# Sixteen-head attention and routed experts: VectorE adds the rotation products itself, and the row maximum is split around the additions

## The reference

```
xn = layernorm(x)
q = rope((xn  @ Wq.T + bq) as 16 heads of 8)
k = rope((ctx @ Wk.T + bk) as 16 heads of 8)
v = (ctx @ Wv.T + bv) as 16 heads of 8
p = softmax(where(mask, q k^T / sqrt(8), -1e9))
x = x + tanh(g_x) * ((p v) @ Wo.T + bo)

xn = layernorm(x);  e = argmax(xn @ Wr + br);  g = softmax(...)[e]
x = x + tanh(g_f) * g * (gelu(xn @ W1[e] + b1[e]) @ W2[e] + b2[e])
```

## Time and profile before

| | |
|---|---|
| median of 3 runs | 280.02 us (279.95 to 280.26) |
| the profiled execution, its own time | 283.1 us |
| span from first to last instruction | 281.2 us |
| busy: TensorE, VectorE, ScalarE, GpSimd | 83%, 68%, 59%, 65% |
| mean granted TensorE clock | 0.983 |

### The profile page before, as it was taken

The page is one execution under the profiler, slowest core; times in us unless marked ns, Lnnn a source line. Parts: engine busy times, 40 slices in busy tenths (PEclk is TensorE's granted clock), DMA queues, the critical chain, the costliest instruction groups (busy, mean ns, idle before and its releaser), DMA issues.

```text
span 281.2 us, 10499 instructions
## 1 busy us (share of the span) xinstructions
PE 234.1 (83%) x3529; PEld 203.5 (72%) x3529; DVE 191.5 (68%) x639; ACT 167.2 (59%) x484; POOL 182.7 (65%) x222
## 2 busy tenths in 40 slices
PE   1357898989799898787897899588889999999992
PEld 1235777878578777666776787477778899999992
DVE  5545777888789979998778977868568434434430
ACT  1235678878577787666886777626473434444440
POOL 7374755757646889746988687660747727747645
PEclk9999999999799999999999999979999999999998
DMA  7711355618445464512525122133204423321100
GB/s 217 229 37 28 86 156 148 175 30 213 104 100 145 115 157 115 147 27 40 145 53 148 36 48 47 30 82 100 65 34 139 122 73 91 96 80 41 51 20 20
DMA packets 58535, 26.63 MB, mean 95 GB/s; under 512 B 38608, under 2 KB 53989, under 8 KB 58484
## 3 DMA queue, kind: packets, MB, share of 16 engines
q1 hardware_dynamic: 55204, 20.15, 29.3%
q0 software_dynamic: 2272, 4.46, 4.7%
q10 hardware_dynamic: 1008, 1.35, 1.6%
HBM read 16.70 MB, written 5.51 MB: 79 GB/s over the span
## 4 chain that ended last, share of the span: by engine, by line
PE 48%; DVE 16%; POOL 11%; issue 8%; DMA 6%; ACT 5%; SPq 3%; POOLq 1%; DVEq 0%; ACTq 0%
PE ps L760 13%; PE ps L803 5%; DMA kbd<-kT 4%; PE ps L741 3%; PE ps L818 3%; PE ps L743 3%; PE ps L742 3%; DVE mx L1252 3%; SPq L407 3%; POOL rot L548 2%; POOL rot L542 2%; PE ps L793 2%; PE ps L779 2%; POOL rot_s L544 2%; POOL stk L527 2%
## 5 line engine op out<-in xcount | busy, mean ns | idle before, releaser
L565 POOL DMA_INDIRECT out<-fin,got x39 | 38.1, 978 | 23.8 <-issue 13.0
L1252 DVE TENSOR_REDUCE mx<-ps 128x16 f16<-128x1024 f32 x32 | 39.1, 1222 | 16.5 <-PE ps L818 16.3
L513 POOL DMA_INDIRECT rows<-x_all,dest_i x32 | 33.3, 1041 | 20.3 <-DVE x_all L1080 9.7
L760 PE MATMUL ps<-w_f,hT 128*128 x312 | 44.6, 286 | 0.0
L803 PE MATMUL ps<-vx,pr 128*64 128x32 f32 x1024 | 37.4, 228 | 4.4 <-DVE on L1180 2.4
L803 PEld LDWEIGHTS ps<-vx,pr 128*64 128x64 f32 x1024 | 33.8, 142 | 8.2 <-issue 2.9
L760 PEld LDWEIGHTS ps<-w_f,hT 128*128 128x128 f32 x312 | 37.8, 191 | 0.8
L601 ACT ACTIVATE pr<-ps 128x1024 f32<-128x1024 f32 x32 | 32.8, 1024 | 9.2 <-PE ps L845 8.7
L542 POOL TENSOR_TENSOR rot<-qk,cf 128x256 f32<-128x256 f32 x32 | 23.5, 735 | 22.4 <-ACT qk L623 15.8
L1310 DVE SCALAR_TENSOR_TENSOR fin<-ps,got 128x128 f32<-128x128 f32 x39 | 13.7, 351 | 35.0 <-PE ps L760 35.0
L527 POOL TENSOR_TENSOR stk<-rot,stk 128x256 f16<-128x256 f32 x32 | 21.8, 682 | 23.9 <-DVE stk L1264 23.9
(11 more groups left out here) (161 smaller groups left out, 586.2 us busy)
## 6 DMA issues: line engine op xcount, KB each, us to landing
kbd<-kT SPq DMA_DIRECT2D x128, 32.0 KB
got<-rows SPq DMA_DIRECT2D x39, 72.0 KB, 1.9
w_f<-in_W_rows SPq DMA_DIRECT2D x8, 256.0 KB, 3.0
w_r<-in_W_last_row SPq DMA_DIRECT2D x8, 256.0 KB, 3.9
w_f<-in_L_ffn_W SPq DMA_DIRECT2D x8, 256.0 KB, 5.3
x_all<-in_x SPq DMA_DIRECT2D x3, 512.0 KB, 4.8
xt_all<-in_x_t SPq DMA_DIRECT2D x3, 512.0 KB, 4.3
ct_all<-in_ctx SPq DMA_DIRECT2D x3, 512.0 KB, 4.5
```

What stands on the lines that cost most here:

```text
L513: pool.indirect_dma_start(out=rows, out_offset=bass.IndirectOffsetOnAxis(ap=dest_i[:, t:t + 1], axis=0), in_=x_all[:, t, :], in_offset=Non ...
L565: pool.indirect_dma_start(out=out_d, out_offset=bass.IndirectOffsetOnAxis(ap=got_i[:, u % GOT, R_ID:R_ID + 1], axis=0), in_=fin[:, u % FRI ...
L760: mm = pe.matmul(o, hT[:, par, c, :], w2_f[:, bass.ds(e, 1), c, :].rearrange("p o n -> p (o n)"), start=False, stop=(c == FC - 1))
L1252: dve.tensor_reduce(mx[:, t % 2, 0:H], ps_s[:, :].rearrange("p (h k) -> p h k", k=S), AX.X, ALU.max).then_inc(mx_done, 1)
```

## The change

GpSimd's sum goes to a buffer of its own, `turned`, and serves only the low halves; L527 waits for it. VectorE no longer waits for that sum: it waits for the two products, and makes the high halves by two tensor_tensor additions of 256 columns that read `rot` and `rot_s`, add in fp32 and write fp16. The row maximum becomes two operations of 512 columns (eight heads each), one ahead of the two additions and one behind them. TensorE signals the scores twice, after four and after eight matmuls; `mx_done` counts to two for each tile, and all that waits for the maximum waits for both halves.

```diff
--- before.py
+++ after.py
@@ -172,6 +172,7 @@
         qk = sb("qk", [P, 2, 2 * D])
         rot = sb("rot", [P, 2, 2 * D])
         rot_s = sb("rot_s", [P, 2, 2 * D])
+        turned = sb("turned", [P, 2, 2 * D])
         WIN = 2 * H * STK + 8
         stk = sb("stk", [P, 2, WIN], F16)
         kT = sb("kT", [P, 2, NA, P], F16)
@@ -520,9 +521,10 @@
                 t = i - 1
                 if live(t):
                     par = t % 2
+                    pool.wait_ge(rope_done, t + 1)
                     pool.wait_ge(hi_done, 2 * t + 2)
                     wait(pool, stk_done, t - 1)
-                    f = rot[:, par, :].rearrange("p (h d) -> p h d", d=HD)
+                    f = turned[:, par, :].rearrange("p (h d) -> p h d", d=HD)
                     win = heads(stk[:, par, :], 0, 2 * H)
                     pool.tensor_tensor(win[:, :, 16:24], f, win[:, :, 8:16], ALU.subtract).then_inc(lo_done, 1)
                 if i == max(GROUP_AT):
@@ -545,7 +547,7 @@
                                        qk[:, par, :].rearrange("p (h c two) -> p h c two", c=HD // 2, two=2)[:, :, :, ::-1],
                                        sin_p, ALU.mult).then_inc(rope2, 1)
                     pool.wait_ge(rope2, t + 1)
-                    pool.tensor_tensor(rot[:, par, :], rot[:, par, :], rot_s[:, par, :], ALU.add).then_inc(rope_done, 1)
+                    pool.tensor_tensor(turned[:, par, :], rot[:, par, :], rot_s[:, par, :], ALU.add).then_inc(rope_done, 1)
                 if i in RSTD_AT:
                     rstd_of(RSTD_AT[i])
                 if i in GROUP_AT and i < max(GROUP_AT):
@@ -732,7 +734,7 @@
 
                 e, par = experts[u], u % 2
                 if u == 0:
-                    pe.wait_ge(mx_done, T)
+                    pe.wait_ge(mx_done, 2 * T)
                 pe.wait_ge(f_lo, u + 1)
                 for c in range(FC):
                     o = bank[2 + par][:, P * c:P * c + P]
@@ -812,13 +814,14 @@
                     s = t % RING
                     pe.wait_ge(kbd_ld[s], (t // RING) * 64 + 64)
                     pe.wait_ge(qT_ev, t + 1)
-                    wait(pe, mx_done, t)
+                    wait(pe, mx_done, 2 * t)
                     for a in range(NA):
                         for b in range(2):
                             mm = pe.matmul(ps_s[S * b:S * b + S, 2 * P * a:2 * P * a + 2 * P], qT[:, s, a, S * b:S * b + S],
                                            kbd[:, s, :, 2 * a + b, :, :].rearrange("p w h k -> p w (h k)"),
                                            start=True, stop=True)
-                    mm.then_inc(s_done, 1)
+                        if a % 2 == 1:
+                            mm.then_inc(s_done, 1)
                 t = i - 5
                 if live(t):
                     if t == 0:
@@ -863,7 +866,7 @@
                     second_layer(i - F0 - 2)
                 t = i - 2
                 if live(t):
-                    pe.wait_ge(mx_done, t + 1)
+                    pe.wait_ge(mx_done, 2 * t + 2)
                     pe.wait_ge(qT_ev, min(T, t + 2))
                     wait(pe, mxT_ev, t)
                     pe.transpose(ps_mx, mx[:, t % 2, :], ident_h).then_inc(mxT_done, 1)
@@ -1247,22 +1250,29 @@
                     route_count(after)
                 t = i - 2
                 if live(t):
-                    dve.wait_ge(s_done, t + 1)
                     wait(dve, mxT_done, t - 1)
-                    dve.tensor_reduce(mx[:, t % 2, 0:H], ps_s[:, :].rearrange("p (h k) -> p h k", k=S), AX.X, ALU.max
+                    dve.wait_ge(s_done, 2 * t + 1)
+                    dve.tensor_reduce(mx[:, t % 2, 0:H // 2], ps_s[:, 0:512].rearrange("p (h k) -> p h k", k=S), AX.X, ALU.max
                                       ).then_inc(mx_done, 1)
                 t = i
                 if live(t):
                     par = t % 2
-                    dve.wait_ge(rope_done, t + 1)
+                    dve.wait_ge(rope1, t + 1)
+                    dve.wait_ge(rope2, t + 1)
                     wait(dve, stk_done, t - 1)
                     win = heads(stk[:, par, :], 0, 2 * H)
-                    f = rot[:, par, :].rearrange("p (h d) -> p h d", d=HD)
-                    q_f, k_f = (f[:, w * H:w * H + H, :].rearrange("p h (o d) -> p h o d", o=1).broadcast_to([P, H, 2, HD])
-                                for w in range(2))
-                    dve.tensor_copy(win[:, 0:H, 0:16].rearrange("p h (c d) -> p h c d", c=2), q_f).then_inc(hi_done, 1)
-                    dve.tensor_copy(win[:, H:2 * H, :].rearrange("p h (c d) -> p h c d", c=4)[:, :, 1:4:2, :], k_f
-                                    ).then_inc(hi_done, 1)
+                    def halves(a, w):
+                        f = a[:, par, :].rearrange("p (h d) -> p h d", d=HD)
+                        return f[:, w * H:w * H + H, :].rearrange("p h (o d) -> p h o d", o=1).broadcast_to([P, H, 2, HD])
+                    dve.tensor_tensor(win[:, 0:H, 0:16].rearrange("p h (c d) -> p h c d", c=2), halves(rot, 0), halves(rot_s, 0),
+                                      ALU.add).then_inc(hi_done, 1)
+                    dve.tensor_tensor(win[:, H:2 * H, :].rearrange("p h (c d) -> p h c d", c=4)[:, :, 1:4:2, :], halves(rot, 1),
+                                      halves(rot_s, 1), ALU.add).then_inc(hi_done, 1)
+                t = i - 2
+                if live(t):
+                    dve.wait_ge(s_done, 2 * t + 2)
+                    dve.tensor_reduce(mx[:, t % 2, H // 2:H], ps_s[:, 512:1024].rearrange("p (h k) -> p h k", k=S), AX.X, ALU.max
+                                      ).then_inc(mx_done, 1)
                 if i == 3:
                     dve.memset(c_h[:, :], 0.0).then_inc(s_cz, 1)
                     dve.memset(b2_f[:, :], 0.0).then_inc(s_zb, 1)
```

## The result

The changed kernel takes 300.5 us (median of 4 runs), the kernel before 280.1 in the same series; the ratio of their runs is 1.070, interval 1.065 to 1.074. It is slower by 7.0%, some 19.5 us by that ratio and 20.3 by the two medians. The profiled execution took 299.8 us (span 298.0) against 283.1 (281.2) before, which is 16.7 more. The two profiled executions are not alike in TensorE's clock: the one before ran at a granted clock of 0.50 from 74 to 77 us and again from 183.5 to 186, the one after only from 127 to 130. Their mean granted clocks are 0.983 and 0.994. The one before lay 3.0 us over its median, the one after 0.6 under its own.

What follows compares the result with a forecast made beforehand. The prediction saw a loop through VectorE, TensorE and GpSimd, the next projection waiting for the whole maximum. Step losses summed to 16.0 us, 13.3 without the lock; taking 15, 280.0 + 15 = 295.0 us, range 286 to 300.

Steps and rivals of the forecast that it cites:

- TensorE's wait at L869 is now for the second half ... It had no slack: TensorE's transpose of the maximum: 0.50 us later from the same scores, 0.77 where VectorE's list sets the start.
- the floor of 5.00: Rotation path through additions and second half of the maximum to the next q: at least 5.00 us in every step.
- the price of an addition: VectorE's additions of 256 columns: 0.42 us each, 0.35 from start to start.
- the weights steps at 5.66: Twelve steps with a weights or lock-caught operation ahead of the maximum: GpSimd's sum goes first, period 5.66; 8.6 us in all.
- If VectorE is waiting, it gets in first (0.03 after the release against 0.08 for L548): Lock after the second product: a waiting VectorE addition starts before GpSimd's sum, which comes later at no cost.
- rival 5: GpSimd's sum goes ahead of the additions in plain steps too: 0.66 times 8 more, 300 us; chance 0.05.
- The eight plain steps: Steps 2, 4, 5, 8, 17, 23, 26, 29: a 5.00 us minimum period lifts four of them, 1.3 us together.
- seven steps bound by VectorE's list: Steps 13, 15, 19, 20, 21, 27, 28, where VectorE's list sets the maximum's start: together 5.0 us longer.
- Steps 3 and 30: Steps with long VectorE lists, grouped with step 31: 0.36 us longer each, 1.1 for the three.
- Rival 1: Faster: the low halves' path ahead of the stack transposes counts, 0.5 us net in some 17 steps, 271 us; chance 0.05.
- Rival 4: TensorE's clock falls in more steps after longer standstills, about 3 us each, 301 to 304 us; chance 0.10.
- About 0.2% can be told from no change.: Measurement of the whole kernel: a difference of about 0.2% was said to be distinguishable from none.

Runs made afterwards that it cites:

- experiment 8: The kernel before with TensorE's transpose of the maximum moved behind the next projection; 281.5 us, 1.000.
- experiment 7: The changed kernel with TensorE's transpose of the maximum moved behind the next projection; 285.1 us, 1.012.
- experiment 1: The kernel before with only the split and order of the change: half a maximum, the two casts of GpSimd's sum, half a maximum; 294.7 us, 1.046.
- experiment 2: The changed kernel with the second half of the maximum moved ahead of the two additions; 284.7 us, 1.007.
- experiment 5: The changed kernel without GpSimd's sum, low halves made from the first product (output not the reference's); 287.3 us, 1.021.
- experiment 6: The changed kernel without GpSimd's sum and with casts of the first product for the additions (output not the reference's); 279.5 us, 0.993.
- experiment 12: The changed kernel with a 64-column GpSimd memset just ahead of the sum, behind its wait for the second product; 301.6 us, 1.071.
- experiment 11: The changed kernel with a 64-column GpSimd memset ahead of the sum's wait for the second product; 301.5 us, 1.068.
- experiment 10: The changed kernel with both maximum halves ahead of the additions and TensorE's transpose of the maximum behind the next projection; 284.3 us, 1.010.
- experiment 3: The kernel before with the maximum as two halves, both ahead of the casts; 281.5 us, 0.997.
- experiment 9: The kernel before with both maximum halves ahead of the casts and TensorE's transpose of the maximum behind the next projection; 281.0 us, 0.999.

## Why the prediction was right, and where it was off

The forecast was 295.0 in a range of 286 to 300, 15 us slower; measured were 300.5 and 19.5 to 20.3. The sign and the cause held. The size is off: the time lies half a microsecond beyond the upper end of the range, and the loss is a third more than the likeliest value.

The sum over the steps, 16.0, is close to the 16.4 of the profiled executions, and that is luck. The plain steps grew by 6.2 more than summed, the two other large groups by 3.4 and 2.7 less, and the errors cancel. The loss by the medians is larger than either. A good part of that is the two stretches at half clock that the profiled execution before held. The first is in step 12, which took 7.90 there, and 6.01 in experiment 8, whose trace has no such stretch in it: an estimate of 2 us from these two. The forecast took the 3.1 us over the median off the total, yet let step 12 grow by only 0.5 from its 7.90, and took 15 for its sum of 16.0. How the clock ran in the median executions before is not on record.

- *Step: "TensorE's wait at L869 is now for the second half ... It had no slack".* Right, and shown by experiment 7; experiments 1 and 2 show it from the side of VectorE. In 24 of the 29 steps from 2 to 30 the next q comes 1.20 to 1.26 after the second half's end. In steps 2 and 4 it comes 2.00 and 1.81 after it, in the changed kernel and in experiment 5 alike, which the floor of 5.00 left out.
- *Step: the price of an addition, 0.42, and 0.35 from start to start.* Measured 0.41 to 0.43 where nothing holds it, and 0.34. The half maxima: 0.68 and 0.61, as said.
- *Step: the rotation path as a floor of 5.00.* Right where nothing holds the additions: 5.03 in experiment 5.
- *Step: the weights steps at 5.66.* Measured 5.59 to 5.61 in ten of the twelve. The 0.06 are small pieces: the second addition starts 3.38 after q for the 3.41 summed, and the second half 0.33 to 0.34 after it for 0.35. The group falls short mostly in steps 6 and 18, which grew by 0.3 together in place of 1.0.
- *Step that failed: "If VectorE is waiting, it gets in first (0.03 after the release against 0.08 for L548)".* The 0.03 was read between L548's end and the cast; behind the second product the addition starts 0.08 to 0.09 after its end, which is 0.01 behind the sum. So GpSimd's sum goes first in the plain steps as well. The 0.03 belongs to what is waited for and not to VectorE: in experiment 6 a cast that waits for the second product starts 0.09 after it as well. So the sum did not start 0.7 to 0.8 late in plain steps, as forecast, but 0.07 to 0.09 after the product in every step. That was rival 5, given 0.05. The eight plain steps grew by 7.5 us in place of 1.3. In five of them (5, 8, 17, 23, 29) the period is 5.59 to 5.65, and 5.01 to 5.07 in experiment 5, where there is no sum: 0.58 a step for being 0.01 late. Steps 2 and 4 carry 0.57 of it on top of their longer way to the next q. Step 26 grew by 1.17 for another reason: the lock caught short operations of VectorE's list ahead of the first half, L993 above all, which took 0.24 in the kernel before:

```profile
163.63 1.63 DVE L993 TENSOR_TENSOR logit<-x_all 128x56 f32<-128x56 f32 x1
```

  Experiment 12 shows that the order of the starts decides. It also shows that a right reading of the 0.03 would not have saved the plain steps: with VectorE first, the sum still gets in between the two additions, and the period is 5.55.
- *Step over-sized: seven steps bound by VectorE's list, 5.0 us.* They grew by 1.6. The order and the prices are as said (step 13: 4.69 for the end of the second half, 3.96 before, 0.73). But the lists of steps 20 and 27 got shorter: short operations that had been caught by GpSimd's work run free, or nearly so, in the new rhythm. L1021 in step 27 takes 0.18; as L1018 it had taken 1.15 in that step of the kernel before, and 1.70 in step 20. VectorE's timeline of step 27:

```profile
169.63 0.35 DVE L1193 SCALAR_TENSOR_TENSOR qk<-ps,rstd,bq_bc 128x128 f32<-128x128 f32 x1 [0.72 <-PE ps L782]
...
171.25 0.18 DVE L1021 SCALAR_TENSOR_TENSOR cand<-ldif,cf 128x56 f32<-128x56 f32 x1
...
172.31 0.68 DVE L1255 TENSOR_REDUCE mx<-ps 128x8 f16<-128x512 f32 x1
```

The first half starts 2.68 after q; the maximum had started 3.85 after it. That is luck of the phase and no property of the change; step 26 had the opposite luck.
- *The rest.* The twelve weights steps grew by 5.9; without step 12, whose fall of the clock in the trace before hides some, by 6.9, where 8.1 were summed. Steps 3 and 30 grew by 1.4 in place of 0.7. Altogether 1.6 + 5.9 + 7.5 + 1.4 = 16.4.
- *The two rules of the Trainium skill.* The Trainium skill ("GPSIMD Engine Reference", Specifications) names the contention, and the runs agree: the addition of 0.41 takes 0.99 beside a sum. The Trainium skill ("VectorE: DVE Perf Modes", Mode 2×_2P) says that a tensor_tensor can't use the two-port mode. 0.41 against the cast's 0.29 for the same 256 columns agrees; experiment 6 puts 2.8% on the dearer operation.
- *Rival 1 (faster by the low halves' path)* saw the path rightly: L795 no longer waits. It is just not the last to be ready. *Rival 4 (clock)* came in part. TensorE stood still for 1.60 us before L872 in step 19 of the changed kernel, and behind that its granted clock was 0.50, the 1.2 GHz level:

```profile
127.00:130.00 3.00, 3.00 (x39) 2.53 (x39) 2.08 (x8) 1.51 (x5) 1.95 (x3) 0.50 0.84 279
```

  Steps 19 and 20 take 6.67 and 6.12 there, and 6.35 and 5.90 in experiment 11, which has the same order on VectorE and no such stretch in them: an estimate of 0.5 us. The other three runs of the changed kernel had mean granted clocks of 0.984, 0.978 and 0.959 and took 299.9, 301.0 and 303.0 us. So the clock may account for the half microsecond beyond the range, but not for the loss: the run at 0.994 took 299.8. Standstills of 2.60 and 2.27 us in the same trace (before 39.04 and 168.48) were followed by no fall.
- *"About 0.2% can be told from no change."* Too fine: the interval of the result is 0.4% to either side, and the kernel before took 279.6 to 283.5 us in the series of experiments 6, 10 and 11.

## What to carry to other kernels

Before an operation is split around others so that the first part starts sooner, look who waits for the last part: here TensorE's next projection did, with next to no slack, so what was put between the halves went into the loop. An operation that is handed from GpSimd to VectorE and has two SBUF inputs should be checked against what GpSimd runs beside it; here both engines were released by the same product, and in the plain steps they met within 0.01 us. And a loop in which two paths are equally long gives nothing for the repair of one of them (experiment 3), while a longer path counts at once (experiment 1). A move that is meant as a repair can bring a wait of its own (experiments 7 to 9): look at the list of waits before reading its time.

## What the runs showed of the hardware that was not expected

- The lock between VectorE's additions (two SBUF inputs) and GpSimd's tensor operations goes to the one that starts first, if only by 0.01 us (112.11 against 112.12), for one instruction. It passes to the waiting engine between two instructions of the other (sum 0.93, second addition 0.95 in experiment 12).
- A GpSimd memset of 64 columns did not hold the addition: in experiment 12 it started at 112.64, the addition at 112.67, and the addition took its usual 0.43.
- A held VectorE addition of 256 columns ended 0.27 to 0.29 after GpSimd's operation, less than its own 0.41. Part of its start may run while it is held; no run shows that part by itself.
- A cast of 256 columns takes 0.29 and an addition 0.41 in the same place.
